# Mamba and mixture-of-experts block: routing weight on the input of two more experts, and an earlier routing chain

## The reference, cut to what matters

```
h = layernorm(x) * (1 + ca) + sa
x = x + ga * (h + mamba_forward(norm(h)) + mamba_backward(norm(h)))   # 256 inner channels, 16 states, two directions
h = layernorm(x) * (1 + cb) + sb
w = softmax of the top 2 of (h @ gate_w), else 0                      # [512 tokens, 8 experts]
x = x + gb * ( sum over e of w[:, e] * ((silu(h @ w1[e]) * (h @ w2[e])) @ w3[e]) + shared expert )
```

## Time and profile before

| | |
|---|---|
| median of 3 runs | 2393.27 us |
| the profiled execution | 2398.73 us |
| its span, first to last instruction | 2396.9 us |
| DVE busy | 93% of the span |
| PE busy | 85% |
| POOL busy | 84% |
| ACT busy | 63% |

### The profile page before, as it was taken

One profiled execution on the slowest core, in us unless ns is written; L12 is line 12 of the kernel. 1 busy time (PEld: TensorE's weight loads), 2 busy tenths in 40 slices (PEclk: granted clock), 3 DMA queues, 4 the chain that ended last, 5 costly groups with the idle time before them and its releaser, 6 DMA issues. The chain is left out here.

```text
span 2396.9 us, 31820 instructions
## 1 busy us (share of the span) xinstructions
PE 2026.4 (85%) x9957; PEld 1283.8 (54%) x9957; DVE 2236.7 (93%) x3546; ACT 1504.6 (63%) x2483; POOL 2021.7 (84%) x1334
## 2 busy tenths in 40 slices
PE   6678988879798888988889798888988888897868
PEld 2445655545565555555545465555555555455544
DVE  4999999999999999999999999999999999999962
ACT  4656666676666666666666666666666666666633
POOL 2777989989898998989989898998989889897855
PEclk7688999999999898999999999998999999999999
DMA  5333433433343333334433343343433333343310
GB/s 148 138 137 124 148 130 128 144 130 136 129 147 134 121 138 134 142 126 145 137 127 132 133 142 134 134 141 118 142 134 140 131 133 137 126 138 131 137 59 27
DMA packets 124060, 312.41 MB, mean 130 GB/s; under 512 B 19700, under 2 KB 46308, under 8 KB 123892
## 3 DMA queue, kind: packets, MB, share of 16 engines
q1 hardware_dynamic: 123892, 310.39, 37.5%
HBM read 303.74 MB, written 6.60 MB: 129 GB/s over the span
## 5 line engine op out<-in xcount | busy, mean ns | idle before, releaser
L504 POOL TENSOR_TENSOR bt<-v,bb 128x1024 f32<-128x1024 f32 x511 | 1205.3, 2360 | 93.8 <-DVE psA L942 72.4
L942 DVE TENSOR_TENSOR_SCAN psA<-psA,bt 128x512 f32<-128x512 f32 x1024 | 1198.1, 1217 | 49.3 <-ACT psA L689 42.4
L689 ACT ACTIVATE psA<-dt,aneg 128x512 f32<-128x512 f32 x1024 | 688.4, 688 | 685.2 <-DVE g L952 684.0
L1209 PEld LDWEIGHTS psY<-ident,g 128*128 128x128 f32 x4096 | 491.6, 147 | 504.5 <-DVE g L952 281.2
L1209 PE MATMUL psY<-ident,g 128*128 128x128 f32 x4096 | 590.1, 286 | 198.1 <-DVE g L952 197.9
L952 DVE TENSOR_TENSOR g<-psA,cb 128x512 f32<-128x512 f32 x1024 | 675.0, 679 | 0.0
L602 POOL TENSOR_TENSOR act<-pf,gf 128x512 f32<-128x512 f32 x288 | 366.8, 1274 | 112.2 <-DVE pf L1046 90.7
L1318 PE MATMUL F<-h2T,w 128*128 128x512 f32 x576 | 334.0, 664 | 112.4 <-DVE pf L1046 110.7
L1364 PE MATMUL F<-w,act 128*128 128x128 f32 x2304 | 298.0, 276 | 4.4 <-POOL act L602 3.1
L1364 PEld LDWEIGHTS F<-w,act 128*128 128x128 f32 x2304 | 276.7, 192 | 14.8 <-POOL act L602 11.0
L1225 PE MATMUL psP<-xnT,wcT 128*128 128x512 f32 x496 | 238.6, 604 | 0.0
(11 more groups left out here) (184 smaller groups left out, 1922.5 us busy)
## 6 DMA issues: line engine op xcount, KB each, us to landing
bb<-bc_rows SPq DMA_DIRECT2D x256, 512.0 KB, 3.7
cb<-bc_rows SPq DMA_DIRECT2D x256, 512.0 KB, 3.6
wB<-w_rows SPq DMA_DIRECT2D x80, 256.0 KB, 4.1
x<-in_L_attn_x SPq DMA_DIRECT2D x16, 256.0 KB, 4.4
out_x<-osb SPq DMA_DIRECT2D x16, 256.0 KB, 4.3
modA<-mod_table SPq DMA_DIRECT2D x15, 192.0 KB, 4.1
w<-in_L_ffn_ew SPq DMA_DIRECT2D x2, 1024.0 KB, 7.2
bc_rows<-xd SPq DMA_DIRECT2D x32, 64.0 KB, 3.0
```

Source lines behind the costliest of these rows:

```text
L504: g.tensor_tensor(bt[:, n % 2, :, :], v[d][:, :, :], bb[:, n // 2 % 2, n % 2, :].unsqueeze(1).broadcast_to([P, NH, T]), ALU.mult).then_inc ...
L689: s.activation(psA[:, half * T:half * T + T], dt_[d][:, half, :], ACT.Exp, scale=aneg[d][:, half, n:n + 1]).then_inc(a_s, 1)
L942: w.tensor_tensor_scan(ah, ah, bt[:, n % 2, half, :][:, order], 0.0, ALU.mult, ALU.add)\
L1209: last = m.matmul(psY[:, half * T + i * P:half * T + i * P + P], g_[:, n % 2, half, i * P:i * P + P], ident[:, :], is_transpose=True, star ...
```

## The change

SCALED goes from 4 to 2: only e = 1 is still weighted on its output by DVE; e = 2 and 3 get the weight on their input like the others, with xs in slots 12 and 14. The routing chain is moved up: exponential in ACT's slot 8 ahead of that slot's other work, the sum gs in POOL's slot 8, the reciprocal in DVE's slot 8, the weights in POOL's slot 9, the transposition in slot 10, the store of w_rows in SP's slot 11 and the first two broadcasts of wB in SP's slot 12. The router logits are read in PSUM, without the copies gl and gl2. v of the backward direction moves from slot 14 to slot 11. In the last pass the downs have slots of their own, up to slot 30.

```diff
-V_SLOT = (30, 14)
+V_SLOT = (30, 11)
-SCALED = 4
+SCALED = 2
-TURN_SLOT, ROWS_SLOT = 13, 14
-XS_SLOTS = {16: 4, 18: 5, 20: 6, 22: 7, 24: 8}
+TURN_SLOT, ROWS_SLOT = 10, 11
+XS_SLOTS = {12: 2, 14: 3, 16: 4, 18: 5, 20: 6, 22: 7, 24: 8}
...
+TAIL_DOWN_SLOTS = [slot for slot in range(10, 31) if slot not in (12, 13, 23)]
-def downs_at(slot):
+def downs_at(fb, slot):
-    return [divmod(k, 2) for k, at in enumerate(DOWN_SLOTS) if at == slot]
+    return [divmod(k, 2) for k, at in enumerate(TAIL_DOWN_SLOTS if fb == NB - 1 else DOWN_SLOTS) if at == slot]
...
 POOL, ffn_side:
-                if slot == GATE_SLOT + 2:
+                if slot == GATE_SLOT + 1:
                     pool.wait_ge(ge_s, fb + 1)
                     g.tensor_tensor(gs[:, :], ge[:, :], ones[:, :], ALU.add).then_inc(gw_s, 1)
-                if slot == GATE_SLOT + 4:
+                if slot == GATE_SLOT + 2:
                     expert_weights(fb)
...
 ACT, body, ahead of expert_turns and exps (before: in ffn_side, behind them):
+                    if ffn and slot == GATE_SLOT + 1:
+                        act_e.wait_ge(gate_s, GATES * (b - 1) + GATE_D)
+                        s.activation(ge[:, :], gd[:, :], ACT.Exp).then_inc(ge_s, 1)
...
 DVE, gate:
-                w.tensor_copy(gl[:, :, :], F2[:, 0:NT * NX]).then_inc(gate_s, 1)
-                dve.wait_ge(gate_s, q + 1)
-                w.tensor_copy(gl2[:, :, :], F2[:, 0:NT * NX]).then_inc(gate_s, 1)
                 for i in range(NT):
-                    w.max(top[:, i, :], gl[:, i, :]).then_inc(gate_s, 1)
+                    w.max(top[:, i, :], F2[:, i * NX:(i + 1) * NX]).then_inc(gate_s, 1)
...
                 for i in range(NT):
-                    w.max_index(topi[:, i, :], top[:, i, :], gl2[:, i, :]).then_inc(gate_s, 1)
+                    w.max_index(topi[:, i, :], top[:, i, :], F2[:, i * NX:(i + 1) * NX]).then_inc(gate_s, 1)
...
 DVE, ffn_side:
-                if slot == GATE_SLOT + 3:
+                if slot == GATE_SLOT + 1:
                     gate_weights(fb)
```

More of the change, by code:

```diff
@@ L186, in adaln_mamba_moe @@
         h2T = sb("h2T", [D, T])
-        gl = sb("gl", [P, NT, NX])
-        gl2 = sb("gl2", [P, NT, NX])
         top = sb("top", [P, NT, NX])
@@ L295, in adaln_mamba_moe @@
         out_d = sem("out_d")
-        GATES = 14
-        GATE_D = 12
+        GATES = 12
+        GATE_D = 10
         LARGE, SMALL, FFN_LOADS = 16 * 5, 16 * 10, 16 * 7
@@ L790, in ffn_side @@
                         .then_inc(F2_free, 1)
-                if slot == GATE_SLOT + 1:
-                    act_e.wait_ge(gate_s, GATES * fb + GATE_D)
-                    s.activation(ge[:, :], gd[:, :], ACT.Exp).then_inc(ge_s, 1)
                 if slot == TURN_SLOT:
@@ L797, in ffn_side @@
                     s.activation(wtsT[:, :], psP[0:NX, :], ACT.Copy).then_inc(wtsT_s, 1)
-                if (0, 1) in downs_at(slot):
+                if (0, 1) in downs_at(fb, slot):
                     act_e.wait_ge(F2_full, (DOWN + NE) * fb + DOWN + 1)
@@ L1012, in gate @@
                 dve.wait_ge(F2_full, (DOWN + NE) * fb + GATE + 1)
-                w.tensor_copy(gl[:, :, :], F2[:, 0:NT * NX]).then_inc(gate_s, 1)
-                dve.wait_ge(gate_s, q + 1)
-                w.tensor_copy(gl2[:, :, :], F2[:, 0:NT * NX]).then_inc(gate_s, 1)
                 for i in range(NT):
-                    w.max(top[:, i, :], gl[:, i, :]).then_inc(gate_s, 1)
-                dve.wait_ge(gate_s, q + 6)
+                    w.max(top[:, i, :], F2[:, i * NX:(i + 1) * NX]).then_inc(gate_s, 1)
+                dve.wait_ge(gate_s, q + 4)
                 w.tensor_copy(topv, top[:, :, 1]).then_inc(gate_s, 1)
                 for i in range(NT):
-                    w.max_index(topi[:, i, :], top[:, i, :], gl2[:, i, :]).then_inc(gate_s, 1)
-                dve.wait_ge(gate_s, q + 7)
+                    w.max_index(topi[:, i, :], top[:, i, :], F2[:, i * NX:(i + 1) * NX]).then_inc(gate_s, 1)
+                dve.wait_ge(gate_s, q + 5)
                 wait(dve, ge_s, fb)
                 w.tensor_tensor(gd[:, :], topv, top[:, :, 0], ALU.subtract).then_inc(gate_s, 1)
+                dve.wait_ge(gate_s, q + 9)
+                w.tensor_copy(topf, topi[:, :, 0:2]).then_inc(gate_s, 1)
                 dve.wait_ge(gate_s, q + 11)
-                w.tensor_copy(topf, topi[:, :, 0:2]).then_inc(gate_s, 1)
-                dve.wait_ge(gate_s, q + 13)
                 wait(dve, wts_s, 3 * fb)
@@ L1049, in expert_sum @@
             def expert_sum(fb, slot):
-                ends = [e for e, part in downs_at(slot) if part]
+                ends = [e for e, part in downs_at(fb, slot) if part]
                 for e in [e for e in ends if 0 < e < SCALED]:
@@ L1350, in ffn_late @@
                     last.then_inc(F2_full, 1)
-                for e, part in downs_at(slot):
+                for e, part in downs_at(fb, slot):
                     if part == 0:
```

## The result

| | kernel before | changed kernel |
|---|---|---|
| median of 4 runs | 2393.4 us (2392.3 to 2395.4) | 2543.0 us (2540.2 to 2544.5) |
| span of the profiled execution | 2396.9 us | 2541.2 us |
| busy DVE, PE, POOL | 2237, 2026, 2022 us | 2201, 2076, 2060 us |

The changed kernel takes 1.0616 times as long (95% interval 1.0602 to 1.0629), 149.6 us more. Forecast were +113 us, 2506, within 2465 to 2547.

What follows compares the result with a forecast made beforehand. DVE was taken to bound the passes with scans, provided POOL's bt arrives. Per pass 9.15 + 1.4 - 2.98 = +7.57 us, 113.6 over 15 passes, +113 with the tail: 2506 us, range 2465 to 2547.

Steps and rivals of the forecast that it cites:

- The stall at scan 14: xs of e = 2 in POOL's slot 12 waits for wB behind cb, holding bt of step 14: 9.15 us a pass.
- The landing: Time for a wB issued right behind a cb to land, within the scan 14 wait: 4.1 us, ends 3.0 to 6.2.
- v: v in POOL's slot 11 stands ahead of bt of step 13: scan 13 stalls 1.4 us a pass, ends 0 to 2.4.
- What DVE loses: DVE sheds eight L1059 instructions (2.24 us), gate copies (0.34) and waits for bt (0.4): 2.98 us a pass gained.
- PSUM reads: DVE's eight reads of the router logits from PSUM cost nothing extra; upper end 0.7 us a pass.
- The tail: Last pass: spread downs gain 1.5 us, delayed acts cost 0.3 to 0.9; net -0.5 us, ends -1.5 and +3.
- rival 1: wB's rows land before POOL reaches xs, so POOL is not held: 2369 us, or 2348 without v's stall; chance 4%.
- rival 2: wB's rows wait only for the store of w_rows, not for cb: +32 us, 2425 us; chance 3%.
- Rival 3: TensorE falls to 1.2 GHz in every stall and tf adds a us or two: +144, 2536 us; chance 10%.

Runs made afterwards that it cites:

- experiment 2: Changed kernel with SP issuing the first two wB ahead of bb and cb in slot 12: 2421.7 us, 1.0096 of the kernel before.
- experiment 3: Changed kernel with w_rows stored in SP's slot 10 and the first two wB issued in slot 11: 2404.4 us, 1.0033 of the kernel before.
- experiment 1: Changed kernel with SCALED = 4, so e = 2 and 3 are weighted on the output again: 2396.6 us, 0.9997 of the kernel before.
- experiment 11: Changed kernel with SCALED = 4 and v of the backward direction in slot 14: 2383.7 us, 0.9947 of the kernel before.
- experiment 5: Changed kernel with v of the backward direction back in slot 14: 2556.5 us, 1.0658 of the kernel before.
- experiment 7: Kernel before with DVE's eight L1059 instructions for e = 2 and 3 replaced by two one-column settings: 2390.1 us, 0.9968 of the kernel before.
- experiment 8: psP ahead of downs on PE, slots 17 and 18: kernel before without facc of e = 2, 3, 2389.1 us; changed kernel with w_rows/wB in slots 10/11, 2405.8.
- experiment 9: Kernel before without DVE's facc of e = 2 and 3, and with a quarter of their downs' matmuls on PE: 2383.0 us, 0.9943.
- Experiment 10: Kernel before with only the logits read in PSUM and the last pass's downs spread: 2390.3 us, 0.9972 of the kernel before.

## Why the prediction was right, and where it was off

**The stall at scan 14** was right in place, order and nearly in size. Forecast were 0.03 + 0.37 + 4.1 + 4.86 = 9.36 us from read-out 13 to scan 14; measured 0.03 + 0.41 + 4.46 + 4.83 = 9.73. The landing was the term that was short: 4.4 us in this pass (4.2 to 4.6 in the others), where the 4.1 were of another wB behind a cb. Over all passes scan 14 waited 145.2 us, 9.68 a pass, 9.47 more than the 0.21 before, where 9.15 were forecast: 5 us more in all. Experiments 2 and 3 show the cause: with the same instructions in another order on SP the loss falls from 148 to 23 and to 8 us. The 2.6 us that the prediction worked out from the Trainium skill (DMA: Bandwidth & Descriptors, anatomy of one DMA) lie below every landing here (3.0 to 6.2). That section gives its figures for transfers that GpSimd issues on the software path. These were issued by SP, so it was no price for them.

**v** was right: a stall at scan 13 of 1.24 us against 1.4. Without the two experts, v in slot 11 costs 12 us against v in slot 14 (experiments 1 and 11), less than the 21 forecast for it; with them it is worth 10 us to leave it in slot 11 (experiment 5), since slot 14 is then full as well.

**What DVE loses** is where the sum went wrong, in the term of 8 x 0.28 = 2.24 us a pass. It was taken at full value because DVE is busy for 93% of the span, and nothing was put down for waits that would take its place. Experiment 7 cashes 7.7 of 30 us, 0.5 a pass, and in the changed kernel the same two waits grew. In spans of the two profiled executions:

| us in all | forecast | measured |
|---|---|---|
| waits for bt | +152 | +160.3 |
| waits for psP and tf | 0 | +29.9 (19.4 and 10.5) |
| DVE busy | -39 | -36.1 |
| waits for the decay factors | 0 | -5.0 |
| all other idle time of DVE, tail included | -0.5 | -4.8 |
| span | +113 | +144.3 |

The forecast of bt is 15 x (9.15 + 1.4) - 5.9, that of DVE's work 15 x (2.24 + 0.34). The waits for psP and tf are nearly the whole difference of 31 us. By the medians it is 37: the execution of the kernel before that was profiled lay 5.3 us above its median, that of the changed kernel on it.

In slots 17 to 21 PE is busy without a gap, which fits these waits; this is one of five such stretches from 1330 to 1350 us of the changed kernel, columns as above:

```profile
1334.00:1338.00 4.00, 4.00 (x24) 2.75 (x23) 3.03 (x4) 1.91 (x4) 4.00 (x3) 1.00 0.46 178
```

Which part of PE's work holds DVE is open: its order is not the cause (experiment 8), less of it gave back some 6 us, with POOL's bt behind it in some passes and a lower clock in others (experiment 9). The few small waits of the earlier trace rows had told that DVE was not held up. They had not told how little later the others were.

**PSUM reads** at no extra cost: right. A maximum takes 155 ns from PSUM, an index search 164; with the copies in SBUF they took 153 and 161. Experiment 10 gives 6.7 us, by its trace in the passes and not in the tail.

**The tail**: from the start of the last pair of scans to the end of the span there were 2396.9 - 2309.14 = 87.8 us, and now 2541.2 - 2455.35 = 85.9. A gain of 1.9 against 0.5, but not where it was forecast: 1.5 of it lie ahead of DVE's first read of the router logits, where the change does nothing (25.8 us from the last scans to it, and now 24.4; 24.4 too in experiment 7, with the same code there as before). From there to the last facc it takes 55.5 us before and 55.4 now: the facc starts 1.2 us sooner behind the last act, as the spread downs were to make it, but that act ends 1.1 us later.

**Rivals.** 1 and 2 needed wB ahead of read-out 13; experiment 2 is rival 2 built, and gave +23 us where its working had said +32. Rival 3 came nearest in time (2536 against 2543) and is wrong in its cause: the clock does fall to 1.2 GHz in each stall, but the waits for tf are nearly the same without the stall (46.7 and 44.8 us, experiment 3). In slot 17 the clock does cost something once PE idles ahead of it (experiments 5 and 9).

## What to carry to other kernels

A wait costs what stands behind it on its engine, not what it guards: before an instruction is put on a queue that feeds the bound engine, follow its operand back through every queue, and if one of them waits for the bound engine itself, the whole way round lies bare. Look at the issuing queue too, where a transfer that has been ready for long can stand behind one that is not. And a saving on an engine that is busy for 93% need not be worth its full length: take the work out alone first (experiment 7) and see what it brings before paying for it on engines at 85%.

## What was not expected of the hardware

A broadcast of 256 KB issued 0.4 us behind one of 512 KB landed after 4.2 to 4.6 us (the first wB of slot 12, changed kernel), and one with nothing issued for 2.7 us or more ahead of it after 3.1 to 3.5 (experiment 2). With less work for PE in slots 16 to 19, the clock granted to it around slot 17 fell in eight of 15 passes (to 0.59 to 0.69 over four us), and its result came 0.6 us later there than with all of the work (1.60 and 0.96 us of waiting, experiments 9 and 7). MAX8 and FIND_INDEX8 of eight elements cost 2 to 3 ns more from PSUM than from SBUF.
